# Recurrent block and resampler: ScalarE adds the token mixes' constants, and five engines get new orders

## The reference, cut to what matters

```python
xa = _ln(x, ln1_w, ln1_b)
sx = concatenate([state, xa[:, :-1]]) - xa
t = tanh((xa + sx * maa_x) @ maa_w1).reshape(B, L, 5, -1)
m = einsum('blfd,fdc->blfc', t, maa_w2)          # five mixes
xw = xa + sx * (maa_w + mw)                       # and xk, xv, xr, xg alike
w = exp(-exp(time_decay + tanh(xw @ decay_w1) @ decay_w2))
r, k, v, g = xr @ Wr.T, xk @ Wk.T, xv @ Wv.T, silu(xg @ Wg.T)
# per head and step: out = r . (faaaa * k v^T + s);  s = k v^T + w * s
y = group_norm(out) * gn_w + gn_b
x = x + (y * g) @ Wo.T
# then a second token shift and the channel mix:
x = x + sigmoid(xr2 @ fWr.T) * (square(relu(xk2 @ fWk.T)) @ fWv.T)
```

## Time and profile before

| | |
|---|---|
| runs of the kernel before | 906.09, 907.30, 912.79 us; median 907.3 us |
| profiled execution | 907.18 us, span 905.4 us |
| busy over the span | TensorE 857.8 us (95%), VectorE 567.1 us (63%), ScalarE 429.4 us (47%), GpSimd 228.5 us (25%) |
| scan instructions of VectorE | 128, from 36.1 to 367.5 us |
| attention's first scores on TensorE | 417.9 us |

### The profile page before, as it was taken

The page is one execution under the profiler, slowest core; times in us unless marked ns, Lnnn a source line. Parts: engine busy times, 40 slices in busy tenths (PEclk is TensorE's granted clock), DMA queues, the critical chain, the costliest instruction groups (busy, mean ns, idle before and its releaser), DMA issues.

```text
span 905.4 us, 16349 instructions
## 1 busy us (share of the span) xinstructions
PE 857.8 (95%) x6220; PEld 671.0 (74%) x6220; DVE 567.1 (63%) x1318; ACT 429.4 (47%) x965; POOL 228.5 (25%) x242
## 2 busy tenths in 40 slices
PE   6777999999999988999999999999989999999998
PEld 5766777686867765676787777877767677888987
DVE  3499999999999989552233453333434365544654
ACT  3313242424242445344666685757656885333342
POOL 3546556464646458200000000000000000110100
PEclk9988999999999999999999999999999999999999
DMA  7657645554637253104002020202140231000200
GB/s 272 164 117 207 186 138 148 147 150 134 158 114 189 81 153 78 49 19 106 18 9 86 9 63 1 63 1 63 30 185 1 105 133 64 1 0 0 82 0 35
DMA packets 44421, 80.51 MB, mean 89 GB/s; under 512 B 21485, under 2 KB 27629, under 8 KB 42558
## 3 DMA queue, kind: packets, MB, share of 16 engines
q1 hardware_dynamic: 39742, 77.71, 29.8%
q10 hardware_dynamic: 4608, 1.84, 0.8%
HBM read 70.36 MB, written 9.18 MB: 88 GB/s over the span
## 4 chain that ended last, share of the span: by engine, by line
PE 46%; ACT 3%; DMA 1%; issue 1%; DVE 1%; SPq 0%; DVEq 0%
PE bank L1856 9%; PE bank L1843 8%; PE bank L1717 8%; PE bank L1723 7%; PE bank L1809 4%; PE bank L1801 3%; PE bank L1828 3%; PE bank L1765 2%; PE bank L1751 2%; ACT smb L1300 2%; DMA cx<-latc_scratch 1%; ACT pts L1308 1%; PE bank L1475 0%; PE bank L1817 0%; ACT cx_hi L1190 0%
## 5 line engine op out<-in xcount | busy, mean ns | idle before, releaser
L900 DVE CUSTOM_DVE_ANT_0 smb<-bank,mask 112x487 f32<-112x487 f32 x128 | 78.1, 660 | 126.1 <-issue 126.0
L693 DVE TENSOR_TENSOR_SCAN scan<-bank,scan 128x448 f32<-128x448 f32 x128 | 132.0, 1073 | 5.8 <-POOL scan L547 4.9
L1481 PEld LDWEIGHTS bank<-xj,front 128*128 128x128 f32 x1024 | 119.6, 196 | 10.1 <-issue 8.1
L544 POOL TENSOR_TENSOR scan<-scan,ks 128x896 f32<-128x896 f32 x64 | 124.2, 1940 | 2.3 <-DMA scan<-v_scratch 2.2
L1481 PE MATMUL bank<-xj,front 128*128 128x112 f32 x1024 | 121.9, 280 | 1.5 <-POOL xj L535 1.5
L1300 ACT ACTIVATE smb<-smb,nmax 112x487 f32<-112x487 f32 x128 | 88.3, 691 | 64.9 <-DVE nmax L900 64.5
L521 POOL TENSOR_TENSOR small<-small,neghalf 112x1 f32<-112x1 f32 x24 | 13.4, 559 | 362.4 <-DVE small L936 268.1
L700 DVE TENSOR_TENSOR scan<-scan,bank 128x896 f32<-128x896 f32 x64 | 68.8, 1078 | 1.8 <-PE bank L1481 1.0
L535 POOL TENSOR_TENSOR xj<-tmp,xa 128x448 f32<-128x448 f32 x40 | 42.4, 1062 | 86.1 <-DVE tmp L662 86.1
L1121 ACT ACTIVATE bank<-ws 128x448 f32<-128x448 f32 x32 | 17.5, 548 | 91.1 <-DVE scan L693 77.2
L1809 PE MATMUL bank<-ident,smb 112*122 112x112 f32 x512 | 56.6, 262 | 3.9 <-ACT smb L1300 3.5
(11 more groups left out here) (196 smaller groups left out, 1760.8 us busy)
## 6 DMA issues: line engine op xcount, KB each, us to landing
scan<-v_scratch SPq DMA_DIRECT2D x64, 448.0 KB, 5.5
cx<-in_ctxt SPq DMA_DIRECT2D x8, 750.0 KB, 5.2
raw_w<-in_wbig SPq DMA_DIRECT2D x4, 1024.0 KB, 7.8
w<-in_w SPq DMA_DIRECT2D x2, 2048.0 KB, 7.4
w<-in_w SPq DMA_DIRECT2D x1, 3328.0 KB, 11.7
tail<-in_wbig SPq DMA_DIRECT2D x3, 1024.0 KB, 9.2
front<-in_wbig SPq DMA_DIRECT2D x2, 1024.0 KB, 9.9
x_f<-in_x SPq DMA_DIRECT2D x8, 224.0 KB, 6.3
```

What stands on the lines that cost most here:

```text
L544: g.tensor_tensor(buf[:, :, :], buf[:, :, :], ks[b % 2][:, k:k + 1, 0:T].broadcast_to([P, VS, T]), ALU.mult).then_inc(s["a_ready"], 1)
L693: n = v.tensor_tensor_scan(flat, decay, flat, 0.0, ALU.mult, ALU.add)
L900: v.tensor_tensor_reduce(sm[r], bank[r][0:T, 0:NKEY], mask_b[b % 2][:, :], -1.0 / DH, 3e38, ALU.add, ALU.min, nmax[:, h:h + 1]).then_inc(s ...
L1481: i = t_.matmul(tiles(dst)[:, m, :], w[:, k, m * P:(m + 1) * P], x[:, k, :], start=k == 0, stop=k == NT - 1)
```

## The change

ScalarE gets a new function, `share`: it reads a mix from PSUM, adds the constant, and writes the slot of `tmp`. VectorE's `mix` is one product in place, over all four groups.

```diff
+            def share(d, j):
+                act.wait_ge(s["m_ready"], d * NMIX + j + 1)
+                if j >= 2:
+                    act.wait_ge(s["xj_ready"], d * NMIX + j - 1)
+                columns(tmp[:, j % 2], tiles(MIX_BANK[j]), None, "maa_" + "vkwrg"[j], "share_ready")
...
             def mix(d, j):
-                dve.wait_ge(s["m_ready"], d * NMIX + j + 1)
-                if j >= 2:
-                    dve.wait_ge(s["xj_ready"], d * NMIX + j - 1)
-                for k in range(NT):
-                    i = v.scalar_tensor_tensor(out=tmp[:, j % 2, k, :], in0=tiles(MIX_BANK[j])[:, k, :],
-                                               scalar=V["maa_" + "vkwrg"[j]][:, k:k + 1], in1=sx[:, k, :],
-                                               op0=ALU.add, op1=ALU.mult)
-                i.then_inc(s["mix_ready"], 1)
+                dve.wait_ge(s["share_ready"], d * NMIX + j + 1)
+                v.tensor_tensor(tmp[:, j % 2], tmp[:, j % 2], sx[:, :, :], ALU.mult).then_inc(s["mix_ready"], 1)
 
             def own_token(b):
                 dve.wait_ge(s["pr_ready"], b + 1)
                 dve.wait_ge(s["ks_ready"], b + 1)
+                wait(dve, "y_ready", b)
```

Of the diff of the orders, TensorE's first half:

```diff
             def period(i):
                 if i == -1:
                     spare_products(12)
-                if i == 0:
-                    sum_pair(0, 0)
+                if 0 <= i - 1 < B - 1:
+                    variances(i - 1)
+                if 0 <= i - 2 < B - 2:
+                    latents_turned(i - 2)
                 if 0 <= i + 1 < B:
                     adapter_inputs(i + 1)
-                if 0 < i < B:
+                if 0 <= i < B:
                     sum_pair(i, 0)
+                    own_sums(i)
                 if 0 <= i + 1 < B:
                     adapters(i + 1, (MIX_V, MIX_K, MIX_W))
                 if i == -1:
                     spare_products(10)
                 if 0 <= i < B:
-                    own_sums(i)
+                    sum_pair(i, 1)
                 if 0 <= i - 1 < B - 1:
                     block_output(i - 1)
-                if 0 <= i + 1 < B:
-                    value_product(i + 1)
                 if i + 1 == B:
                     kv(0, 0)
                 if 0 <= i + 1 < B:
+                    value_product(i + 1)
                     key_product(i + 1)
                 if 0 <= i - 1 < B - 1:
                     second_turned(i - 1)
```

More of the change, by code:

```diff
@@ L400, in period @@
                 if 0 <= i < B:
+                    store_values(i)
+                    chunk(i, 0)
+                    chunk(i, 3)
+                    chunk(i, 1)
                     chunk(i, 2)
-                    chunk(i, 3)
+                    chunk(i, 5)
+                if i == 2 + NT:
+                    output_bias()
+                    sp.wait_ge(s["pad_ready"], 1)
+                    load_context(0)
+                if 0 <= i < B:
                     chunk(i, 4)
-                    chunk(i, 5)
-                if 0 < i + 2 < B:
+                if 0 <= i - 3 < B - 2:
+                    store_columns(i - 3)
+                if 1 <= i + 2 < B:
                     load_input(i + 2)
@@ L415, in period @@
                     attention_weight(i - 2)
[L416 to L419, removed]
+                if 0 <= i < B:
+                    chunk(i, 6)
                 if 0 <= i - 2 < B - 1:
                     store_latents(i - 2)
+                if 1 <= i - 1 < B:
+                    load_residual(i - 1)
+                if i == B - 1:
+                    load_context(1)
                 if 0 <= i < B:
-                    chunk(i, 6)
                     chunk(i, 7)
@@ L781, in period @@
             def period(i):
+                if 0 <= i + 1 < B:
+                    shift(i + 1)
+                if 0 <= i < B:
+                    scan_chunk(i, 0)
+                    scan_chunk(i, 1)
+                if 0 <= i + 1 < B:
+                    shifted(i + 1)
+                if 0 <= i - 1 < B:
+                    whole_y(i - 1)
+                if i == 2:
+                    dve.wait_ge(s["wg_turned"], 1)
+                    v.memset(cx[0][:, :, NKEY:PAD], 0.0).then_inc(s["pad_ready"], 1)
+                if 0 <= i < B:
+                    scan_chunk(i, 2)
+                    scan_chunk(i, 3)
+                if 0 <= i - 2 < B - 1:
+                    gated_values(i - 2)
+                if 0 <= i - 1 < B:
+                    centred(i - 1)
+                if 0 <= i < B:
+                    times_r(i, 0)
+                if 0 <= i - 2 < B - 1:
+                    latents(i - 2)
                 if 0 <= i < B:
                     times_r(i, 1)
-                if 0 <= i + 1 < B:
-                    shifted(i + 1)
-                if 0 <= i < B:
+                    own_token(i)
                     times_r(i, 2)
@@ L805, in period @@
                 if 0 <= i < B:
+                    scan_chunk(i, 4)
+                if 0 <= i + 1 < B:
+                    mix(i + 1, MIX_V)
+                if 0 <= i < B:
+                    scan_chunk(i, 5)
                     own_values(i)
@@ L1194, in period @@
                 if 0 <= i < B:
-                    decays(i, 0)
+                    decay_tanh(i)
+                    share(i, MIX_R)
+                    share(i, MIX_G)
+                    decay_logs(i)
                 if 0 <= i - 2 < B - 1:
@@ L1208, in period @@
                 if 0 <= i < B:
+                    decays(i, 0)
+                    decays(i, 1)
+                if 0 <= i - 2 < B - 1:
+                    second_gate(i - 2)
+                if 0 <= i < B:
                     decays(i, 2)
@@ L1226, in period @@
                 if 0 <= i + 1 < B:
-                    values(i + 1)
-                    store_second_values(i + 1)
+                    share(i + 1, MIX_V)
+                    share(i + 1, MIX_K)
+                    share(i + 1, MIX_W)
+                if i + 1 == 0:
+                    turned_weight("Wg", "wg_loaded", "wg_turned")
                 if 0 <= i < B:
@@ L1660, in period @@
                     second_turned(i - 1)
-                if 0 <= i < B:
-                    sum_pair(i, 1)
                 if 0 <= i + 1 < B:
+                    decay_in(i + 1)
                     adapters(i + 1, (MIX_R, MIX_G))
@@ L1675, in period @@
                     kv(0, 2)
+                if 0 <= i + 2 < B:
+                    input_turned(i + 2)
+                if 0 <= i - 1 < B - 1:
+                    hidden_gate(i - 1)
                 if 0 <= i < B:
```

133 lines of the change are left out of this document (38 added, 95 removed).

## The result

The changed kernel takes 938.5 us (936.79 to 938.84) against 907.8 us of the kernel before on the same chip: ratio 1.0325 (1.0283 to 1.0368), 31 us slower where 6 us faster was forecast. The profiled execution took 938.84 us, span 937.1 us, mean granted clock 0.965 (before 0.989).

What follows compares the result with a forecast made beforehand. TensorE (42.06 us) and VectorE (42.35) nearly fill a 43.1 us period. Start -1.9, sequences 1 to 5 +3.0, sequence 6 +1.4, way to the scores +3.8: 6.3 us gained from 907.3, forecast 901; own range 897.5 to 904.5, wider 895.5 to 909.

Steps and rivals of the forecast that it cites:

- GpSimd's work is unchanged, and SP's transfers too; they are moved past each other.: Middle periods: moving GpSimd's work and SP's transfers within the new order was costed at nothing.
- VectorE's 40.4 us: VectorE's own work per middle period: 43.1 us less a 0.43 us wait, less 2.25 us for the products.
- one under 1.00 in the middle periods: A granted clock below 1.00 in the middle periods, listed as a sign that the forecast is wrong; no size given.
- The start: Stretch up to sequence 1's end: ScalarE's shares delay the first scan; 1.9 us lost, 114.8 against 112.94 us.
- the 37.7 forecast: Start of the kernel: first scan at 37.7 us in place of 36.09.
- 73.4, 114.8, 284.6, and 329.2 + 82.4 = 411.6: Forecast last `sum_pair` starts of sequences 0, 1, 5, 6, then 82.4 us to the attention's first scores.
- the product: VectorE's in-place mix product: 0.52 us in place of 0.97 for four instructions, 2.25 us less per period.
- `hidden_gate`'s 0.34 us for the relu: TensorE between `hidden_keys` and `hidden_gate`: about 0.34 us of waiting per period for ScalarE's relu.
- 0.66 us before the norm end (0.65): VectorE before `norm_end` of the first norm: waits out GpSimd's power, 0.65 us with handoffs per period.
- mixes off the loop: Middle period: none of the five mixes lies on the 43.1 us loop, so with old orders their cut becomes waiting.
- chunk 1 landing late: Slower rival: SP's new order lands chunk 1 late, delaying VectorE's second scan; at 10 us landing 913 us; chance 0.12.
- TensorE's busy time held as a floor: TensorE's 42.06 us per middle period cannot shrink; the rival that it is no floor gave 895 us, chance 0.05.

Runs made afterwards that it cites:

- the forms by themselves: Separate kernel of ten VectorE instruction forms, alone and beside a 2.07 us GpSimd product; the norm-end form took 2051 ns beside it, 537 alone.
- the clock held at 1.00: Changed kernel plus 14 spare TensorE products just before `hidden_keys`, results unused: 941.47 us, ratio 1.0344 to the kernel before.
- the run with two waits: Changed kernel with GpSimd holding scan products 6 and 7 until the norm end beside each is done: 931.36 us, ratio 1.0243 to the kernel before.

## Why the prediction was wrong, step by step

- **The failed step**: "GpSimd's work is unchanged, and SP's transfers too; they are moved past each other." The sum has no term for that move. GpSimd's work is unchanged in amount, but it was moved beside VectorE's norm ends, `shift` and `shifted`. The durations of VectorE's 40.4 us come from rows in which GpSimd stood idle or worked beside PSUM operands. Put beside a product these cost 1.58 + 1.77 us on the norm ends and 0.5 to 1.6 us on `shift` or `shifted` in a period, in two periods 0.6 and 1.2 us on `latents`. Shown from four sides: taking the products away gives 34 us (nothing in the kernel before), keeping them apart gives 25 us, one product put beside rows_t in the kernel before costs 8 us, and the forms by themselves behave so.
- **What it drew after it**: `second_shift` late by those 3.35 us, TensorE dry for 1.7 us, the clock at 0.50, relu and input columns late, 1.4 to 1.7 us of waiting before `shift` in three periods. The prediction had no price for a lower clock, but named one under 1.00 in the middle periods as a sign of being wrong: it was 0.93 to 0.96. With the clock held at 1.00 a period was 46.87 us in place of 47.9 in the mean of four, so it is the smaller part.
- **The start** (9.0 us late by sequence 1) has the same cause. The first scan came at 36.27, better than the 37.7 forecast; then `shifted` took 4.2 us for 1.06, rows_f 2.30 us behind a wait of 1.81 for GpSimd's power, queued behind product 6, and `shift` 2.50 us. Without the products (profiled execution 900.23 us, the fastest of ten) sequences 0, 1 and 5 end at 72.47, 113.93 and 283.64 and the scores come at 410.47: forecast 73.4, 114.8, 284.6, and 329.2 + 82.4 = 411.6.
- **Right**: the product (611 ns busy, two in 1.15 us), `hidden_gate`'s 0.34 us for the relu, 0.66 us before the norm end (0.65), mixes off the loop (new mixes, old orders: 1.0012).
- **The rivals**: chunk 1 landing late was the wrong mechanism for the slow side: VectorE's scans wait 1.1 us in all for GpSimd between 42 and 410 us. TensorE's busy time held as a floor as far as the runs go: without the products TensorE had no bracketed wait, was busy 42.28 of 42.43 us, and weight loads filled only 32.01 us of them. That nothing shorter is possible is not shown, since VectorE with its waits needs nearly as long there (40.41 + 0.66 + 0.97 = 42.04 us). That one engine's time depends on what another does beside it was none of the rivals.
- **Sum**: even without the stall the forecast's kernel gains little: 904.6 us, ratio 0.994, and that with most of GpSimd's multiplication left out.

## What to carry to other kernels

A duration read from a trace holds for what ran beside it there. When a change moves GpSimd's work, list VectorE's instructions that take two inputs from SBUF, or scale one tensor from SBUF to SBUF, and look what GpSimd does at their new place; the profile shows a stall as a long instruction with no wait ahead of it, that ends just behind GpSimd's (0.3 us here). And a GpSimd product in an "idle" gap is not free: one of 2.08 us cost 1.52 us a period here.

## What the hardware showed beside that

- The shutting out is mutual, and in these rows goes by who begins first: VectorE stood 1.5 to 1.8 us behind a product, GpSimd 0.8 us behind VectorE (2.87 for 2.08 us).
- An idle TensorE of 1.69 us was followed by a stretch at clock 0.50; idle times of 1.10 to 1.12 us ahead of the same step, in the run with two waits, were followed by 1.00 in three cases and by 0.68 in the fourth, and a later one of 0.48 us, which 1.1 us of work parted from one of 1.02 us, by 0.68 as well. The length of that one wait alone does not tell.
- GpSimd's product of 128x896 takes 1.78 us for chunks 2 to 5 and 2.09 us for 0, 1, 6 and 7, in the kernel before as in the changed one. That stayed unexplained.
